# Weights issued by ScalarE, a held down product, and routed activations turned through memory

## The reference

```python
x = x + attention(layernorm(x))        # 8 heads of 16, causal, compressed keys and values, rope, exact gelu
n = layernorm(x)
scores = sigmoid(n @ gate_w.T)         # 8 experts
top_scores, top_idx = top_k(scores, 2) # scaled to a sum of 2.5
routed = sum over the two experts of weight * (silu(n @ w1[e]) * (n @ w3[e])) @ w2[e]     # 512 -> 352 -> 512
shared = (silu(n @ sw1) * (n @ sw3)) @ sw2                                               # 512 -> 352 -> 512
x = x + routed + shared
```

## Time and profile before

| | us |
|---|---|
| median of 3 runs | 1528.33 |
| lowest, highest | 1523.52, 1529.8 |
| profiled execution, its own time | 1535.9 |
| its span, first to last instruction | 1534.0 |
| TensorE busy | 1414.4 (92%) |
| VectorE busy | 893.3 (58%) |
| ScalarE busy | 508.8 (33%) |
| GpSimd busy | 452.3 (29%) |
| mean granted TensorE clock | 0.965 |

### The profile page before, as it was taken

How to read it: one execution, slowest core, us unless ns; L and a number is a source line. 1 busy time by engine, 2 the same in 40 slices (tenths; PEclk the granted TensorE clock), 3 DMA queues, 4 the chain that set the end, 5 groups by cost and what they waited for, 6 DMA issues and landing times.

```text
span 1534.0 us, 21932 instructions
## 1 busy us (share of the span) xinstructions
PE 1414.4 (92%) x6059; PEld 704.4 (46%) x6060; DVE 893.3 (58%) x2655; ACT 508.8 (33%) x1042; POOL 452.3 (29%) x431
## 2 busy tenths in 40 slices
PE   6997999999999998899899984699999999999996
PEld 3552223333433332455455542355555555555553
DVE  4898998888788861678687864233333333333331
ACT  4662456766676677212021121011111111111110
POOL 0000000000000000000222252667777777777771
PEclk9996999999999999899899997799999999999998
DMA  7685310310320000466676752244444444444442
GB/s 219 217 237 156 80 39 4 78 43 5 68 58 4 5 5 16 135 195 180 158 174 176 180 101 50 48 67 71 69 69 69 69 69 69 69 70 70 69 69 35
DMA packets 124854, 136.81 MB, mean 89 GB/s; under 512 B 37046, under 2 KB 86590, under 8 KB 124774
## 3 DMA queue, kind: packets, MB, share of 16 engines
q1 hardware_dynamic: 101350, 96.56, 24.4%
q0 software_dynamic: 21520, 37.84, 14.4%
q10 hardware_dynamic: 1904, 1.46, 0.3%
HBM read 87.03 MB, written 48.83 MB: 89 GB/s over the span
## 4 chain that ended last, share of the span: by engine, by line
PE 72%; DVE 13%; DMA 5%; issue 5%; ACT 2%; SPq 1%; POOL 1%; ACTq 0%; DVEq 0%; POOLq 0%
PE psum L1046 28%; PE psum L1057 14%; PE psum L959 8%; PE psum L941 7%; PE psum L923 6%; PE psum L873 3%; DVE arena L1239 3%; DVE psum L1237 2%; PE psum L1029 2%; DMA xq<-xn_rows 2%; DMA xn_rows<-xg 2%; DMA attn_cur<-attn_rows 1%; PE psum L1020 1%; PE psum L944 1%; ACT arena L709 1%
## 5 line engine op out<-in xcount | busy, mean ns | idle before, releaser
L1046 PE MATMUL psum<-arena,xg_t 128*128 (+2 forms) x1648 | 520.1, 470 | 20.5 <-DVE xg_t L1209 19.9
L1046 PEld LDWEIGHTS psum<-arena,xg_t 128*128 128x128 f32 x1648 | 312.4, 195 | 182.8 <-issue 32.9
L781 ACT ACTIVATE arena<-psum 128x512 f32<-128x512 f32 (+3 forms) x640 | 303.6, 535 | 176.2 <-PE psum L941 87.3
L643 POOL DMA_INDIRECT table<-const,slot_i x64 | 62.5, 976 | 865.2 <-DVE slot_i L1424 756.1
L659 POOL DMA_INDIRECT xq<-xn_rows,quad_rows x284 | 272.2, 958 | 96.4 <-issue 88.9
L1057 PE MATMUL psum<-arena,act_t 128*128 (+3 forms) x618 | 282.5, 593 | 1.2 <-ACT act_t L809 0.7
L1239 DVE TENSOR_REDUCE arena<-psum 128x1 f32<-128x512 f32 x384 | 251.0, 685 | 30.5 <-PE psum L923 29.9
L923 PE MATMUL psum<-arena 96*128 96x512 bf16 (+3 forms) x640 | 219.1, 363 | 17.8 <-DVE arena L1237 9.6
L1320 DVE TENSOR_TENSOR act_sb<-psum,silu 128x352 f32<-128x352 f32 x103 | 54.0, 524 | 284.8 <-ACT silu L831 226.9
L941 PE MATMUL psum<-arena 99*128 99x512 bf16 (+3 forms) x640 | 215.0, 353 | 3.5 <-ACT arena L781 2.7
L831 ACT ACTIVATE silu<-psum 128x352 f32<-128x352 f32 x103 | 47.8, 464 | 466.8 <-PE psum L1046 410.5
(11 more groups left out here) (138 smaller groups left out, 894.6 us busy)
## 6 DMA issues: line engine op xcount, KB each, us to landing
arena<-qk_parts SPq DMA_DIRECT2D x48, 256.0 KB, 6.2
arena<-in_w SPq DMA_DIRECT2D x16, 704.0 KB
arena<-in_x SPq DMA_DIRECT2D x32, 256.0 KB, 4.4
x<-in_x SPq DMA_DIRECT2D x32, 256.0 KB
xn_rows<-xg SPq DMA_DIRECT2D x32, 256.0 KB
xq<-xn_rows SPq DMA_DIRECT2D x128, 64.0 KB
out_rows<-y_sb SPq DMA_DIRECT2D x32, 256.0 KB
qk_parts<-arena SPq DMA_DIRECT2D x16, 384.0 KB, 3.2
```

The lines of the kernel that those rows point to most:

```text
L781: nc.scalar.activation(probs[:, at_b % PS, d * P:], psum[:, NA + at_b % NBK, 0:CH - d * P], ACT.Exp, scale=float(HD) ** -0.5).then_inc(s_e, 1)
L1046: i = nc.tensor.matmul(psum[:, bank + k % 2, 0:w], xg_t[:, k % 2, c, :], rhs, start=c == 0, stop=c == DC - 1)
```

## The change

1. The expert weights are issued by ScalarE's queue instead of SyncE's, three parts per expert (the 512 and 192 KB pieces together), spread over the first 28 of the 32 shared steps. ScalarE first waits, as SyncE did, for the attention stores.
2. At the end of the shared stage `down` of the last three tiles is held back: TensorE does `ranks` of group 4, `down` 29, `at` 31, `down` 30, `ranks` of group 5 and `down` 31 after `up` 31. It uses bank 7 for two of them and three buffers of transposed activations. VectorE makes the slots of group 4 after `gated` 31, and `y` 29 to 31 around `block_list`.
3. In the routed stage `at` and its copy by ScalarE go. `gated` writes its result in two instructions in another order, ScalarE stores it to memory (192 KB, rows of 1536 bytes), waits for it to land, and loads it back with four DMAs (48 KB each, pieces of 384 bytes); VectorE turns it with one block transpose. `down` and `y` run two blocks behind `up`, and the scatter three behind the gather's counter.
4. The table `iota_be` of 568 words a partition becomes `iota_b` of 71, broadcast where it is read.

```diff
-COUNT_AT = {12: 0, 20: 1, 27: 2, 29: 3, 31: 4}
+COUNT_AT = {12: 0, 20: 1, 27: 2, 29: 3}
+HELD = 3
+W_STEPS = 28
@@ sync, shared step
-                load_expert(n // 4, n % 4)
@@ gpsimd, routed
-                if n >= 2:
-                    scatter(n - 2)
+                if n >= 3:
+                    scatter(n - 3)
@@ scalar
+                    if part == 2:
+                        act.dma_start(w2[:, e, 0:HC - 1, :], ...)
+                        act.dma_start(w2[0:HL, e, HC - 1, :], ...)
...
+                def turn_gated(n, k):
+                    act.wait_ge(ss["a"], n + 1)
+                    if k >= 2:
+                        act.wait_ge(s_aq[k % 2], QP * used(n, k))
+                    act.dma_start(act_rows[k % 2], act_sb[:, k % 2, :]).then_inc(s_as[k % 2], 16)
+                    act.wait_ge(s_as[k % 2], used(n, k) + 16)
+                    if k >= 2:
+                        act.wait_ge(ss["ate"], n - 1)
+                    w = HP // QP
+                    for i in range(QP):
+                        act.dma_start(aq[i * QW:(i + 1) * QW, k % 2],
+                                      act_rows[k % 2][:, i * w:(i + 1) * w].rearrange("(g a) d -> a g d", g=QP)).then_inc(s_aq[k % 2], 16)
...
-                    if k >= 1:
+                    if ss is sh and k >= 1:
                         at_copy(n - 1, k - 1)
                     if ss is sh:
+                        for i in range(3 * E * n // W_STEPS, min(3 * E, 3 * E * (n + 1) // W_STEPS)):
+                            load_expert(i // 3, i % 3)
...
                     nc.scalar.activation(silu[:, :], psum[:, 1 + k % 2, 0:H], ACT.Silu).then_inc(ss["silu"], 1)
+                    if ss is ro:
+                        turn_gated(n, k)
@@ tensor, step
-                    if k >= 1:
+                    if shared and k >= 1:
                         at(n - 1, k - 1)
                     up(n, k, expert(n))
-                    if k >= 1:
-                        down(n - 1, k - 1, expert(n - 1))
+                    behind = 1 if shared else 2
+                    if k >= behind and not (shared and n - 1 >= NT - HELD):
+                        down(n - behind, k - behind, expert(n - behind))
@@ tensor, after the shared steps
+                    ranks(len(GROUPS) - 2, NT)
+                    down(NT - 3, NT - 3, None)
+                    at(NT - 1, NT - 1)
+                    down(NT - 2, NT - 2, None)
+                    ranks(len(GROUPS) - 1, NT)
+                    down(NT - 1, NT - 1, None)
@@ vector
+                        nc.vector.tensor_tensor(place[:, 0:HC - 1], by_chunk(psum[:, 3 + k % 2, 0:whole], HC - 1),
+                                                by_chunk(silu[:, 0:whole], HC - 1), ALU.mult)
+                        nc.vector.tensor_tensor(place[:, HC - 1, 0:HL // QW], psum[:, 3 + k % 2, whole:H].rearrange("p (i b) -> p i b", b=QW),
+                                                silu[:, whole:H].rearrange("p (i b) -> p i b", b=QW), ALU.mult).then_inc(ss["a"], 1)
...
+                def turn_gated(n, k):
+                    dve.wait_ge(s_aq[k % 2], QP * (used(n, k) + 16))
+                    if k >= 2:
+                        dve.wait_ge(ss["dn"], n - 1)
+                    nc.vector.transpose(act_t[:, k % 2].rearrange("p c (g a) -> p g c a", g=QP),
+                                        aq[:, k % 2].rearrange("p g (c b) -> p g c b", c=HC)).then_inc(ss["ate"], 1)
...
-                    if k >= 1:
+                    if shared and k >= 1 and n - 1 < NT - HELD:
                         y(n - 1, k - 1)
+                    if not shared and k >= 1:
+                        turn_gated(n - 1, k - 1)
+                    if not shared and k >= 2:
+                        y(n - 2, k - 2)
```

More of the change, by code:

```diff
@@ L52 @@
 _at = 0
-for _n, _w in (("ident", P), ("rev8", E), ("first_slot", E), ("iota_be", NB * E),
+for _n, _w in (("ident", P), ("rev8", E), ("first_slot", E), ("iota_b", NB),
                ("quarter", 1), ("own", QP), ("pairs", 2 * TOP_K * NT), ("spare_pairs", 2 * P)):
@@ L401, in program @@
         s_r = sem("route_chain")
+        s_as = [sem(f"gated_rows_stored_{i}") for i in range(2)]
+        s_aq = [sem(f"gated_quarters_loaded_{i}") for i in range(2)]
         s_sel, s_cnt, s_cntr = sem("selected_ready"), sem("ranks_ready"), sem("ranks_read")
@@ L682, in _ @@
                     gather(n + 2)
-                if n >= 2:
-                    scatter(n - 2)
-            scatter(NB - 2)
-            scatter(NB - 1)
+                if n >= 3:
+                    scatter(n - 3)
+            for n in range(NB - 3, NB):
+                scatter(n)
             for i in range(2):
@@ L1050, in down @@
                     pe.wait_ge(ss["ate"], n + 1)
+                    held = shared and n >= NT - HELD
                     if k >= 1:
-                        pe.wait_ge(ss["ye"], n)
+                        pe.wait_ge(ss["ye"], n - 1 if held else n)
+                    out = psum[:, 7 if held and (NT - n) % 2 == HELD % 2 else 6, :]
+                    ring = AT if shared else 2
                     for c in range(HC):
@@ L1056, in down @@
                         rhs = sh2[0:r, c, :] if shared else w2[0:r, bass.ds(e, 1), c, :].rearrange("p a n -> p (a n)")
-                        i = nc.tensor.matmul(psum[:, 6, :], act_t[0:r, k % 2, c, :], rhs, start=c == 0, stop=c == HC - 1)
+                        i = nc.tensor.matmul(out, act_t[0:r, k % ring, c, :], rhs, start=c == 0, stop=c == HC - 1)
                     i.then_inc(ss["dn"], 1)
@@ L1079, in experts @@
                         step(n, n)
+                    ranks(len(GROUPS) - 2, NT)
[4 more added lines that the diff above has]
+                    down(NT - 1, NT - 1, None)
                 else:
                     run_steps(pe, count, step, u)
[L1082 to L1085, removed]
+                    down(count - 2, count - 2, expert(count - 2))
+                    down(count - 1, count - 1, expert(count - 1))
             def ranks(g, turns):
@@ L1334, in y @@
                     if shared:
[L1335 removed]
+                        bank = 7 if n >= NT - HELD and (NT - n) % 2 == HELD % 2 else 6
+                        i = nc.vector.tensor_tensor(y_sb[:, k % 2, :], x1[:, k % XR, :], psum[:, bank, :], ALU.add)
                     else:
@@ L1438, in block_list @@
                 chain(nc.vector.tensor_tensor_scan(ends, blocks, zero, 0.0, ALU.add, ALU.add))
-                chain(nc.vector.tensor_tensor(by_block, over_b(ends), cf("iota_be").rearrange("p (b e) -> p b e", e=E), ALU.is_le))
+                chain(nc.vector.tensor_tensor(by_block, over_b(ends), cf("iota_b").rearrange("p (b a) -> p b a", a=1).broadcast_to([P, NB, E]), ALU.is_le))
                 chain(nc.vector.tensor_reduce(eid, by_block, AX.X, ALU.add))
```

55 lines of the change are left out of this document (36 added, 19 removed).

## The result

| us | before | after |
|---|---|---|
| median (4 runs each, side by side) | 1529.07 | 1554.95 |
| lowest, highest | 1523.52, 1532.72 | 1552.61, 1557.3 |
| ratio, 95% interval | | 1.019 (1.017 to 1.021) |
| span of the profiled execution | 1534.0 | 1555.5 |
| TensorE busy | 1414.4 (92%) | 1408.9 (91%) |

A forecast was written before the change was run, and what follows sets the result against it. It saw three limits: TensorE itself, a chain through routing and the table, and something late in the shared stage. Terms of -1.1, -5, -7, -9, -22 and +4 gave -40 us: median 1488 us, range 1466 to 1532.

The forecast's parts named there:

- the first sum of term 5: ScalarE's loop in a routed block, from `up`'s end through silu, `gated`, store landing and four issues: 5.4 us of 7.32.
- term 5: Steady routed blocks, `up` 2 to `up` 70: 68 steps each 0.32 us shorter, -22 us.
- term 4: Filling of the routed stage: `up` 2 starts earlier, at about 980.4 us; -9 us (-6 or -12 depending on silu 0).
- the last sentence: Signs of being wrong, among them unexplained stalls of ScalarE or TensorE, like silu 0's 5.4 us, falling elsewhere; no chance given.
- 1 constants: Start of the kernel: 254 KB less constants to load before TensorE's first transposes, -1.1 us (0 to -2).
- 2 weights on ScalarE: Shared stage: SyncE's store and loads no longer wait behind queued weights, -5 us (+5 to -13).
- 3 end of the shared stage: Last shared steps: `ranks` moved behind `up` returns 3 us, steps without weights speed store and loads; -7 us (0 to -12).
- 6 draining: End of the routed stage: the last `down` starts near 8 us after the last `up`, +4 us (+3 to +9).
- Rival **C: Shared stage gives nothing, ScalarE's weights crowding the same stores: 1500 us, 1515 with added stalls; chance 0.08.
- Rival **A: Routed stage: ScalarE's round trip binds, costing from a store landing of 4.3 us; 1563 us at 5.4; chance 0.17.
- Rival **B: Routed stage: GpSimd or the scatter's landing takes over; at 7.64 us a block 22 us are lost, 1510; chance 0.10.

The follow-up runs named there:

- the first comparison: Changed kernel against the kernel before, four runs each side by side on an unrecorded chip: 1554.95 us against 1529.07, ratio 1.019.
- traffic added: Kernel before with the same store and four reloads issued by ScalarE in each routed block, nobody reading what they load, on chip 12: 1523.16 us, ratio 1.001.
- eight reloads: Changed kernel with each of the four reloads split into two of 16 partitions, eight issues on ScalarE's queue, on chip 9: 1534.43 us, ratio 1.008.

## Why the prediction was wrong, point by point

**The step that failed** is the first sum of term 5. "From `up`'s end: silu starts 0.20 later" was read in one block and taken for all 71. Where the result was measured silu starts 3.4 us after `up`'s end in the median block, against 0.04 in the kernel before: TensorE's signal comes up to 7.2 us late in every third block, mostly by 5 to 7, and ScalarE's loop is still catching up in the next. The 22 us forecast became a loss of 547.8 - 519.7 = 28: 50 us off. The sign had stood in my rows: silu 0 came 5.4 us late for "remote". I priced it in term 4 and named it in the last sentence, as a stall that might "fall elsewhere", but gave it no rival, no time and no chance. Of the 67 us between forecast and result some 50 are this one thing; without it the same kernel takes 1504.6 us, inside the range.

Not settled: what delays the signals, whether it belongs to a chip or to a session on it, and why the new routed stage meets it every third block (+50 us) and the old one hardly. Blocks of 7.31 us against 7.64, the 384 KB a block, or both, could be it. The added traffic was tried only where nothing is late (chip 12). That the old stage hardly meets it rests on one trace, that of the first comparison. On chip 0 there is none of the kernel before, and its time there, 1538.56 us in one run, is 15 us above that of chips 12, 5, 2 and 9, so it may meet it there more often. That a trace was recorded beside the run leaves the recording itself under suspicion too; the three other executions of the kernel after in the first comparison took as long (1552.6 to 1556.2 us), and whether they were recorded isn't known. All five traces with late silus (the kernel before with one in the shared and one in the routed stage, the others with 21 to 23) come from the unrecorded chip or from chip 0.

Where nothing is late, the forecast was -40 us and the measured change on chip 2 is 1504.62 - 1523.94 = -19. Its terms, from profiled executions, the kernel with the changed shared part alone (chip 12) against the kernel after (chip 2):

| term | forecast | measured |
|---|---|---|
| 1 constants | -1.1 | first `up` of the shared stage ends at 632.5 and 631.3, with before's constants at 633.4 (first comparison) and 629.5 (traffic added): nothing that shows |
| 2 weights on ScalarE | -5 | +7.9 |
| 3 end of the shared stage | -7 | -2 to 0 |
| 4 filling | -9 | -5.1 (14.6 to 9.5) |
| 5 steady blocks | -22 | -22.4 (519.7 to 497.3) |
| 6 draining | +4 | +5.4 (19.1 to 24.5) |

Terms 4 to 6 give -22.1, and the spans of the two executions differ by 1524.0 - 1502.4 = 21.6: the routed stage is accounted for. With 3.8 us for the shared part (1.0025 of 1521.61, the interval 0.9997 to 1.0053) the sum is -18.

**1** was too small to be told. **2** had the wrong sign; its bound of +5 was too tight. I had credited the store with no longer queueing behind weights, and left out that weights on a queue of their own run beside it. Its sign of being right, stores that land in 2 to 4 us after table writes begin, did not come (8.40 and 7.45). **3**: 5 us too much. The kernel without held products spends 334.6 us from first shared to first routed `up`, that with them 334.2: the bound of 0 was the answer. The 3 us that were to come back "whatever the DMAs do" did come back at the start of `up` 31, and 1.8 of them went again at the lower clock, which the term had priced for the two `down` products alone. Rival **C** was right for terms 2 and 3: not 0 but a loss of some 4 to 8 us, inside what it allowed "with added stalls". **4**: the times that it adds give 979.9 and not 980.4, half a microsecond more of gain; in the first comparison `up` 0 to `up` 2 fell from 22.2 to 14.1, near the -9; but 7.7 of those 22.2 were silu 0's lateness. In the two undisturbed kernels with the old routed stage the time is 14.5 and 14.6, so the kernel's own gain is 5. **5** was right in all that it says of the median block: chain of `up` 4.74 and `down` 2.58, ScalarE's loop 5.1 of 7.31, a store landing in 1.9 to 2.0 us at 127 GB/s. Rival **A** named the engine that waited but not the reason: its condition, a landing above 4.3 us, was not seen (from the store's issue to the first reload's it was at most 4.0 us in the blocks of seven traces), and ScalarE's loop was the bound only in the kernel with eight reloads. Rival **B** did not come: GpSimd's idle time before a gather is 0.31 us as before, and TensorE never waits for it. **6** was right.

## What to carry to other kernels

When a time contradicts a sum whose parts the profile confirms, run the *unchanged* kernel on another chip before editing it: six kernels here appeared to cure a fault, and no run had shown that their chips had it. Where a wait has no cause in the profile, look for a second engine that waits for the same signal: whether both are late or one tells the sender from the receiver. A "remote" wait for which no engine was late is a finding even when it occurs once; ask what it would cost if it came every third time, and give that a chance of its own. Moving transfers to an idle queue isn't neutral: it cost 7.9 us here, and the order in which one queue had put them may have been what kept them out of the way of a store that everything waits for. The best kernel of these runs keeps the new routed stage and leaves the weights where they were: 1496.74 us, 0.983 (0.9777 to 0.9872) of before on chip 2, but no gain on chip 0 (1.002, one run).

## What the runs showed of the hardware

- One program, unchanged, took 1504.6, 1510.5, 1554.95 and 1564.2 us in four sessions, while the kernel before went from 1522.8 to 1538.6. The difference isn't the clock of TensorE: a mean of 0.961 to 0.968 in the four traces.
- In the slower two, TensorE's signal that `up` is done is seen up to 7.2 us late about every third block, and register moves of 29 ns on SyncE's queue take up to 718 and 1396 ns. In the kernel before one such signal was seen 4.6 us late by ScalarE and at the same moment by GpSimd.
- After 4.9 us without work TensorE's clock was granted at 0.50, and a shared `up` of 4.95 us took 8.1.
- Pieces of 384 bytes against rows of 1536, and four issues against one, made no difference in blocks where ScalarE had 2.5 us to spare: 1504.6 to 1505.6 us in all four forms, on three chips. Nor did the same 384 KB a block added to the kernel before, 1.0013 (0.9992 to 1.0033).
